# Masked attention's result kept on chip, the second normalisation in place with its scaling on ScalarE, and its store in the gate phase

## What is computed

```python
x = _layernorm(x + self_attention(x, Wq, bq, Wk, bk, Wv, bv, Wf, bf))     # ALiBi bias
x = _layernorm(x + _L0_xattn_ref(x, ctx_1024, ctx_1024, mask))            # masked attention
x = _layernorm(x + _L0_ffn_ref(x, w_gate, w_up, w_down))                  # quantised feed-forward

def _layernorm(x, axis=-1, eps=1e-05):
    m = jnp.mean(x, axis=axis, keepdims=True)
    v = jnp.var(x, axis=axis, keepdims=True)
    return (x - m) / jnp.sqrt(v + eps)
```

## Time and profile before

| | us |
|---|---|
| timed runs before, median of 3 | 3351.57 (3349.05 to 3354.13) |
| the profiled execution, its own time | 3340.55 |
| its span, first to last instruction | 3338.8 |
| TensorE busy in the span | 2672.2 (80%) |
| VectorE busy | 2448.1 (73%) |
| GpSimd busy | 2005.9 (60%) |
| ScalarE busy | 1736.5 (52%) |

### The profile page before, as it was taken

One profiled execution on the slowest core, in us unless ns is written; L12 is line 12 of the kernel. 1 busy time (PEld: TensorE's weight loads), 2 busy tenths in 40 slices (PEclk: granted clock), 3 DMA queues, 4 the chain that ended last, 5 costly groups with the idle time before them and its releaser, 6 DMA issues. The chain is left out here.

```text
span 3338.8 us, 79733 instructions
## 1 busy us (share of the span) xinstructions
PE 2672.2 (80%) x24130; PEld 1439.7 (43%) x24130; DVE 2448.1 (73%) x4668; ACT 1736.5 (52%) x3213; POOL 2005.9 (60%) x1479
## 2 busy tenths in 40 slices
PE   6888658888885768999999999923998989301999
PEld 3444325555553433555555555511444434100444
DVE  7778667777774657888888888856433799785776
ACT  2343237777774324666666666621332676575333
POOL 2343379999995216999999999954000566431000
PEclk9999869999998878999999999966999999755999
DMA  7999924444445543122131131167333677587332
GB/s 248 294 316 305 284 91 138 135 127 133 130 133 162 194 153 93 49 76 66 44 95 51 44 98 41 51 226 247 136 120 127 213 255 247 181 280 316 122 123 82
DMA packets 339973, 519.69 MB, mean 156 GB/s; under 512 B 36181, under 2 KB 169045, under 8 KB 339882
## 3 DMA queue, kind: packets, MB, share of 16 engines
q1 hardware_dynamic: 331594, 500.77, 46.9%
q0 software_dynamic: 2752, 9.44, 0.9%
q10 hardware_dynamic: 5536, 8.40, 0.7%
HBM read 279.61 MB, written 202.67 MB: 144 GB/s over the span
## 5 line engine op out<-in xcount | busy, mean ns | idle before, releaser
L1085 POOL TENSOR_TENSOR cross_plo<-cross_p 128x1024 f16<-128x1024 f32 x448 | 906.4, 2056 | 84.8 <-ACT cross_p L923 80.8
L923 ACT ACTIVATE cross_p<-cross_st 128x512 f32<-128x512 f32 x1024 | 555.9, 595 | 289.5 <-PE cross_st L857 289.5
L998 DVE CUSTOM_DVE_ANT_0 cross_junk<-cross_sc,cross_mb 128x1024 bf16<-128x1024 f32 x512 | 619.3, 1220 | 109.9 <-PE cross_sc L818 101.7
L1085 POOL TENSOR_TENSOR self_plo<-self_p 128x1024 f16<-128x1024 f32 (+7 forms) x512 | 576.7, 1161 | 20.9 <-ACT self_p L923 20.4
L923 ACT ACTIVATE self_p<-self_st,self_strip 128x512 f32<-128x512 f32 (+3 forms) x768 | 414.8, 581 | 150.3 <-PE self_st L855 119.1
L998 DVE CUSTOM_DVE_ANT_0 self_junk<-self_sc,self_strip 128x1024 bf16<-128x1024 f32 (+7 forms) x512 | 371.3, 753 | 142.3 <-PE self_sc L818 137.3
L852 PE MATMUL cross_st<-cross_qa,cross_ka 97*128 97x512 f16 x1024 | 390.5, 381 | 2.4 <-ACT cross_p L923 2.1
L857 PE MATMUL cross_st<-cross_nm,idbig 128*128 128x512 f16 x1024 | 389.9, 381 | 0.0
L818 PE MATMUL cross_sc<-cross_ka,cross_qa 96*128 96x512 f16 x1024 | 311.3, 386 | 21.1 <-DMA cross_ka<-scr_k_hi 16.0
L1900 PE MATMUL d_acc<-wd_hi,d_oh 128*128 128x512 f16 x384 | 146.9, 383 | 210.4 <-DVE d_ol L1938 210.4
L880 PEld LDWEIGHTS cross_o<-cross_vh,cross_p 128*128 128x128 bf16 x4096 | 269.8, 97 | 75.4 <-issue 21.2
(11 more groups left out here) (235 smaller groups left out, 6033.1 us busy)
## 6 DMA issues: line engine op xcount, KB each, us to landing
self_strip<-self_strips SPq DMA_DIRECT2D x68, 516.0 KB, 3.2
v_g<-scr_gate SPq DMA_DIRECT2D x97, 256.0 KB, 3.7
scr_gate<-gt_y SPq DMA_DIRECT2D x96, 256.0 KB, 2.0
scr_h<-v_h SPq DMA_DIRECT2D x96, 256.0 KB, 2.5
j_h<-scr_h SPq DMA_DIRECT2D x48, 512.0 KB, 4.6
m<-in_mask_Bx1xSxS_ik SPq DMA_DIRECT2D x34, 512.0 KB, 7.5
d_o<-scr_o SPq DMA_DIRECT2D x9, 1536.0 KB
scr_up<-v_y SPq DMA_DIRECT2D x48, 256.0 KB, 3.5
```

The lines of the kernel that those rows point to most:

```text
L923: nc.scalar.activation(p32[u % NPR][:, q0:q1], stp[cc % 2][:, 0:q1 - q0], ACT.Exp, bias=bias, scale=SM).then_inc(expd, 1)
L998: nc.vector.tensor_tensor_reduce(junk[slot % 2][:, 0:w], sc[slot % 2][:, 0:w], bias, 1.0, -3e38, ALU.add, ALU.max, qmax[n % 2][:, qt:qt + ...
L1085: nc.gpsimd.tensor_tensor(plo[u % NPR][:, q], p32[u % NPR][:, q], high[:, q], ALU.subtract).then_inc(lo_g, 1)
```

## The change

- Masked attention no longer has a staging tile or a store. VectorE writes the scaled result of each head straight into its place in `rows` (the later `x2`), a tile that now exists from before that phase. The address there depends on the loop index by a division and a remainder.
- The second normalisation works in place in `x2`. It loads x1 only, into five buffers; GpSimd adds it to the rows; ScalarE does the scaling, as an Identity with a scale and a bias column; VectorE makes the bias column (minus mean times reciprocal) and takes the largest value of a group one group later. The epsilon goes into the root as its bias. All loops are written out. The weights' loads are issued by SyncE, behind all x1 loads.
- The store of x2 is in the gate phase, on SyncE, once per token group, behind the store of output tile 6.

```diff
@@ attention_phase
-                    if t == SCALE + 2 and not first:
+                    if causal and t == SCALE + 2 and not first:
                         store(i - 1)
...
-                store(NI - 1)
-                sp.wait_ge(o_out, 16 * NI)
+                if causal:
+                    store(NI - 1)
+                    sp.wait_ge(o_out, 16 * NI)
...
                     dve.wait_ge(o_recip, head + 1)
                     dve.wait_ge(o_read, head * 2 + 4)
-                    if m == 0:
-                        dve.wait_ge(o_out, i * 16)
-                    nc.vector.tensor_tensor(ost[:, :, m * HD:(m + 1) * HD], osum[n % 2][:],
+                    if causal:
+                        if m == 0:
+                            dve.wait_ge(o_out, i * 16)
+                        out = ost[:, :, m * HD:(m + 1) * HD]
+                    else:
+                        w = i if n >= 0 else i - 1
+                        out = kept[:, ds(w // (H // HB) * ST, ST), ds(w % (H // HB) * (HB * HD) + m * HD, HD)]
+                    nc.vector.tensor_tensor(out, osum[n % 2][:],
                                             rden[n % 2][:].unsqueeze(2).to_broadcast([P, ST, HD]), ALU.mult).then_inc(o_scaled, 1)
@@ second_norm_phase
+    TQ, NR, NS = 2, 5, 3
...
+        rows = lambda n: x2[:, n * D:(n + 1) * D]
             @block.sync
+                for g in range(NQ):
+                    if g >= NR:
+                        sp.wait_ge(added, (g - NR) * TQ + TQ)
+                    sp.dma_start(b[g % NR][:], x1_dram[g * (TQ * P):(g + 1) * (TQ * P), :].rearrange("(t p) n -> p t n", p=P)).then_inc(t_in[g % NR], 16)
+                for dst, src in loads:
+                    sp.dma_start(dst, src).then_inc(weights_in, 16)
+                sp.wait_ge(weights_in, 16 * len(loads))
             @block.gpsimd
+                for g in range(NQ):
+                    pool.wait_ge(t_in[g % NR], g // NR * 16 + 16)
+                    for tt in range(TQ):
+                        nc.gpsimd.tensor_tensor(rows(g * TQ + tt), rows(g * TQ + tt), b[g % NR][:, tt], ALU.add).then_inc(added, 1)
             @block.scalar
+                act.wait_ge(eps_set, 1)
+                for g in range(NQ):
+                    j = g % NS
+                    act.wait_ge(aggregated, g * TQ + TQ)
+                    nc.scalar.activation(sd[j][:], mv[j][:, :, 1], ACT.Sqrt, bias=eps[:, 0:1]).then_inc(root, 1)
+                    act.wait_ge(centred, g + 1)
+                    for tt in range(TQ):
+                        nc.scalar.activation(rows(g * TQ + tt), rows(g * TQ + tt), ACT.Identity, scale=rs[j][:, tt:tt + 1],
+                                             bias=nm[j][:, tt:tt + 1]).then_inc(scaled, 1)
             @block.vector
-                    dve.wait_ge(aggregated, g * (TQ + 1) + TQ)
-                    nc.vector.tensor_scalar(mv[v][:, :, 1], mv[v][:, :, 1], EPS, None, ALU.add).then_inc(aggregated, 1)
...
+                def scale(g):
+                    j = g % NS
                     dve.wait_ge(root, g + 1)
+                    nc.vector.reciprocal(rs[j][:], sd[j][:]).then_inc(recip, 1)
                     dve.wait_ge(recip, g + 1)
+                    nc.vector.scalar_tensor_tensor(out=nm[j][:], in0=mv[j][:, :, 0], scalar=-1.0, in1=rs[j][:],
+                                                   op0=ALU.mult, op1=ALU.mult).then_inc(centred, 1)
...
+                for g in range(NQ):
+                    statistics(g)
+                    if g >= 1:
+                        largest(g - 1)
+                    scale(g)
+                largest(NQ - 1)
@@ gate_phase
                             sp.dma_start(y_dram[o, :, ds(g * GT, GT)], y[o % NY][:]).then_inc(stored[o % NY], 16)
+                            if o == FT // 2:
+                                sp.dma_start(token_group(x2_dram, g), x2[:, ds(g * (TG * D), TG * D)].rearrange("p (t n) -> p t n", n=D)).then_inc(x2_out, 16)
@@ decoder_layer
+        rows = Kit(nc, ctx).sb("rows", [P, RES * T], F32)
+        attention_phase(nc, c, "cross", False, q2_dram, k2_dram, v2_dram, None, mb_dram, nm_dram,
+                        kept=rows[:, 0:T // P * D].rearrange("p (t n) -> p t n", n=D))
```

More of the change, by code:

```diff
@@ L1351, in _ @@
-                with act.Fori(0, NQ // NR) as i:
-                    for v in range(NR):
-                        g = i * NR + v
-                        act.wait_ge(aggregated, g * (TQ + 1) + TQ + 1)
-                        nc.scalar.activation(sd[v][:], mv[v][:, :, 1], ACT.Sqrt).then_inc(root, 1)
-                        if v:
-                            store(g - 1)
-                    store(i * NR + (NR - 1))
-                act.wait_ge(x2_out, 16 * NQ)
+                act.wait_ge(eps_set, 1)
@@ L1361, in _, with statistics @@
             @block.vector
             def _(dve):
-                def statistics(g, v):
+                nc.vector.memset(eps[:], EPS).then_inc(eps_set, 1)
+                def statistics(g):
+                    j = g % NS
+                    if g >= NS:
+                        dve.wait_ge(scaled, (g - NS) * TQ + TQ)
                     for tt in range(TQ):
                         dve.wait_ge(added, g * TQ + tt + 1)
-                        nc.vector.bn_stats(st[v][:, tt], a[v][:, tt]).then_inc(stats, 1)
+                        nc.vector.bn_stats(st[j][:, tt], rows(g * TQ + tt)).then_inc(stats, 1)
@@ L1416, in _, with gate_phase @@
                     dve.wait_ge(steps, 2 * j + 2)
-def gate_phase(nc, c, x2, scale, inverse, wts, y_dram, x_dram, gmax, loads):
+def gate_phase(nc, c, x2, x2_dram, scale, inverse, wts, y_dram, x_dram, gmax, loads):
     NY = 3
@@ L1971, in feed_forward @@
         wd = [kit.sb(f"wd_{n}", [P, FT, D], F16) for n in ("hi", "lo")]
-        res = kit.sb("rows", [P, RES * T], F32)
         x2 = res[:, 0:T // P * D]
@@ L1983, in feed_forward @@
                               for j in range(2) for r in range(KT) for k in range(3)]
-                second_norm_phase(nc, attn2, x1_dram, x2, x2_dram, pmax["x"], tiles(wg, 0))
+                second_norm_phase(nc, x1_dram, x2, pmax["x"], tiles(wg, 0))
                 quantisers(nc, "qx", [of("x")])
-                gate_phase(nc, c, x2, scale["x"], inverse["x"], wg, gate_dram, x_dram, pmax["gate"], tiles(wu, 1) + down_tiles)
+                gate_phase(nc, c, x2, x2_dram, scale["x"], inverse["x"], wg, gate_dram, x_dram, pmax["gate"], tiles(wu, 1) + down_tiles)
             quantisers(nc, "qg", [of("gate")])
```

63 lines of the change are left out of this document (19 added, 44 removed).

## The result

The changed kernel took 3368.08 us in the median of six runs (3363.44 to 3369.36); the kernel before, run beside it, 3351.43 (3343.73 to 3355.92). The ratio is 1.0047, with a 95% interval of 1.0035 to 1.0058: slower by half a per cent, where 33.6 us less had been forecast. The profiled execution spans 3364.1 us and took 3365.87.

The account below looks back on a forecast made before the run. TensorE was taken to bound masked attention and the gate phase, VectorE the second normalisation between them. Parts 1 to 4 gave 33.6 us less, parts 5 and 6 nothing: 3351.57 - 33.6 = 3318 us; own range 3311 to 3331, wider 3304 to 3345.

Parts of the forecast that it names:

- Part 6: Masked attention: address work of 0.22 us before each head's write just hidden; value 0, bounds -5 to +100 us.
- rival (a): Masked attention: head writes miss their gap before GpSimd's next instruction; 3389 us if most miss; chance 0.12, partly 0.09.
- the partial case: Masked attention: a third to two thirds of heads miss the gap, 24 to 47 us lost, 3342 to 3365; chance 0.09.
- Part 1: Handover into the second normalisation: with no store due, first loads start 1.12 us after attention's last VectorE instruction; gain 3.3 us.
- Part 2: Second normalisation's first group: half the loads go, landing 4.0 us, first statistics at 2202.9 against 2207.6.
- Part 3: Second normalisation on VectorE: cycle per group 3.24 us for 4.29, plus 5 us of waits; ends at 2263.2, before 2295.5.
- (b): Second normalisation: the two-column instruction waits a full add each time, ScalarE's pair late by 0.3; 3334 us, chance 0.10.
- (c): Second normalisation: the loads set the pace, at worst 4.0 us per group; 3330 us, chance 0.04.
- (d): More gain: no waits on adds in the second normalisation, masked attention 7 us shorter without stores; 3306 us, chance 0.07.
- Part 4: Second normalisation's tail: GpSimd's configuration 1.1 us after VectorE's last instruction, at 2264.3 instead of 2297.9; weight loads hidden.
- Part 5: Gate phase: eight x2 stores of 1 MB hidden behind the gate stores; 0 taken, bounds 0 to 1 us per group.
- Sum: Whole kernel: 33.6 us less, from the second normalisation's end moving from 2297.9 to 2264.3.

Follow-up runs that it names:

- address_moved_ahead: The changed kernel with the head write's address worked out and held in its own register ahead of the reciprocal; 3312.31 us, ratio 0.9899 to the kernel before.
- fixed_place: The changed kernel with every head's result written to one constant place in masked attention, plus one fill of rows before it; 3331.53 us, ratio 0.9944.

## Why the prediction was wrong

**Part 6, the cross phase, is the step that failed**, and within it one term: the address work. It was put at 0.22 us (0.26 at most), from SyncE's same expression, against a margin of 0.24 in the head shown and 0.33 in the median head. Measured, the write came 0.30 later in that head (0.41 to 0.71) although the older wait of 0.09 fell away as foreseen, so the work cost it about 0.39; in the other three it came 0.40, 0.30 and 0.19 later (heads 3, 1 and 2, mod 4). So the work took more than the 0.22 to 0.26 taken in three heads of four, and in two of them (0.39 and 0.40) more than the 0.33 that there was. The recorded durations of the register instructions (0.14 in heads 1 and 2, 0.31 in heads 3 and 0) don't make up these delays alone: even the one of 46 ns in address_moved_ahead goes with 0.10. The margin was read rightly (GpSimd's next instruction still starts at 0.65), and so was what happens behind it: rival (a) came true in its partial form, 29 of 56 heads. But the rival's reason for a part, that TensorE's stall would shift GpSimd's rhythm, did not come true: GpSimd's start stays at 0.65 in all four heads, and it is the arithmetic that differs from head to head. That the partial case's share fitted is luck. Its cost per miss was too low, 1.27 for 1.66. The write ends 2.82 us after the reciprocal instead of 0.97, 1.85 more (2.11 against the 1.889 taken, and 0.30 from the later start beyond the shown head's 0.41); less the cover of 0.28 that is 1.57, and TensorE's waits read 1.49. The remaining 0.1 to 0.2 per miss has no row of its own. So the partial case, given as 24 to 47 us lost and 3342 to 3365, was 48.0 lost and 3368.

The choice that failed was therefore not in the list of causes but in taking the value 0 for a term whose estimate and margin were two hundredths apart, and in the chances: 0.21 for rival (a). With a price from another engine's queue, and an arithmetic that differs in each of the four heads, a number near one half would have been more honest. And the heads should have been read by their place in the iteration: the arithmetic differs in each, so a third outcome, the same two in every four, was the natural one.

**Part 1** held: the first load comes 1.0 us after the last write's end (2252.41 after 2251.43), 1.1 was taken. **Part 2** held: landing and wait of 4.1, first statistics 6.3 us after the last write's end, forecast 6.4.

**Part 3** held in its sum and not in its terms. From the last write's end to that of the final reduction it took 65.6 us (2251.43 to 2317.04), forecast 66.7. The small new instruction waits 0.59 (0.75 against 0.16) where 0.4 was taken, but in ten groups rather than 13; the undisturbed cycle is 3.07, not 3.24. ScalarE's pair (1.52 measured, 1.51 taken) is ready for the reduction in nearly all groups; the root is 0.295 with its bias column, 0.203 without, and once a table load of 1.28 us, which no term had, stands ahead of the first root; the first reciprocal waits 1.71 for that root. The shorter cycle made up for the longer waits and the table load, so that the sum agrees to 1.1 us is in part luck. Rivals (b) and (c) are out: the instruction never waited a full add, and after the first group no load sets the pace. So is the part of (d) in the cross phase: fixed_place has no stores there and takes 884.9 us, for 885.0.

**Part 4** held: the configuration follows 1.1 us after the last reduction (2318.1), and the weights landed 10.9 to 14.6 us after issue at 2283.8, before the stage's end. From the last write's end to the configuration: 66.7 for the forecast 67.8 (2264.3 less 2196.5).

**Part 5**: hidden, as far as can be told. The x2 stores land in 4.3 to 4.5 us, the gate stores in 2.0 to 7.8, and ScalarE's waits for them fell (5.8 us in 3 times, 8.8 in 4 before). The phase reads 273.1 to 276.4 with these stores and 273.3 to 275.1 without, so a cost of one or two us is neither shown nor excluded.

**Sum.** Without the failed term the forecast holds: address_moved_ahead is at 0.9899 of the kernel before (3346.21 in its runs), 33.9 us less, for 33.6 (its 3312 against the forecast's 3318 is the 5 us between the two sets of runs). With it, the traces give 48.0 − 33.3 − 1.0 + 1.5 = +15.2, and the timed medians +16.7.

## What to carry to other kernels

Where two engines that share a path are both full, ask of each instruction between them when it must start, not how long it takes: a few hundredths decide, and they decide for each position of the loop body anew. An address that depends on the loop is work on the engine's own queue, paid just ahead of the instruction that uses it; put it in a register ahead of the last wait, and look in the trace whether it stayed there. When margin and cost are both hundredths and the cost comes from another engine, treat the outcome as open, and give the case on the far side the chance that belongs to a coin.

## What the runs showed of the hardware

- A VectorE instruction that came 0.06 us after GpSimd's start took 2.11 us, one 0.03 ahead of it 0.43. GpSimd's instruction that starts while such a write gets in ahead lasts 2.07 (head 26) to 2.15 us (head 29), for 1.89 alone.
- The delay from register work is more than its recorded duration, and not in proportion: 46 ns went with 0.10 us, 139 ns with 0.19 in one head and 0.30 in another, 312 ns (in two) with 0.39 to 0.40.
- A small instruction can wait as well: 128x2 elements with two tensors as inputs took 0.59 us more in each of the ten groups beside GpSimd's adds, while two 128x1 instructions with one tensor and a column of scalars took 0.34 together, with the adds or without. The 128x512 scaling on VectorE, also of that second form, did lose (2.51 a pair for 1.00).
- A square root on 128x2 took 0.295 us with a bias column, against 0.203 without one.
